# Cross-attention on one core: side work laid out over nearly every key tile, and the scores of a tile behind one wait

## The reference

```
xq  = (1 + scale_q) * layernorm(x)   + shift_q      scale and shift from silu(cond) @ Wss + bss
xkv = (1 + scale_kv)* layernorm(ctx) + shift_kv
q = xq @ Wq + bq                     (4096 x 512, 16 heads of 32)
k, v = xkv @ Wkv + bkv               (3202 x 512 each)
attn = softmax(q @ k^T / sqrt(32))   per head
out = x + (attn @ v) @ Wp + bp
```

## Time and profile before

| | |
|---|---|
| median of 3 runs | 2184.37 us (2181.47 to 2184.44) |
| profiled execution | 2181.79 us, its span 2179.6 us |
| PE busy | 2153.8 us, 99% |
| DVE busy | 1913.6 us, 88% |
| ACT busy | 1817.8 us, 83% |
| exponentials, L1340 | 1600 of 1115 ns, 1692.4 us busy |
| score matmuls, L1091 | 938.3 us busy |
| weigh matmuls, L1103 | 852.3 us busy |

### The profile page before, as it was taken

How to read it: one execution, slowest core, us unless ns; L and a number is a source line. 1 busy time by engine, 2 the same in 40 slices (tenths; PEclk the granted TensorE clock), 3 DMA queues, 4 the chain that set the end, 5 groups by cost and what they waited for, 6 DMA issues and landing times.

```text
span 2179.6 us, 56041 instructions
## 1 busy us (share of the span) xinstructions
PE 2153.8 (99%) x24986; PEld 622.7 (29%) x24986; DVE 1913.6 (88%) x1179; ACT 1817.8 (83%) x1908; POOL 17.3 (1%) x28
## 2 busy tenths in 40 slices
PE   7999999999999999999999999999999999999998
PEld 3444322222222222222222222222222222222222
DVE  2435798899999899999999999999999999989998
ACT  1221899999999999999999999999999999998995
POOL 0001000000000000000000000000000000000000
PEclk9999999999999999999999999999999999999999
DMA  8345522234222422233223322233223322242221
GB/s 297 142 165 181 162 73 56 75 93 115 71 80 77 130 69 77 65 98 109 81 70 99 107 82 69 77 96 106 69 81 89 99 74 77 70 115 83 77 54 51
DMA packets 189011, 210.23 MB, mean 96 GB/s; under 512 B 17238, under 2 KB 120414, under 8 KB 188764
## 3 DMA queue, kind: packets, MB, share of 16 engines
q1 hardware_dynamic: 187180, 206.06, 32.4%
q10 hardware_dynamic: 1584, 0.53, 0.1%
HBM read 169.33 MB, written 37.22 MB: 95 GB/s over the span
## 4 chain that ended last, share of the span: by engine, by line
PE 96%; DVE 1%; issue 1%; ACT 1%; DMA 0%; POOL 0%; SPq 0%; ACTq 0%; DVEq 0%
PE bank L1091 40%; PE bank L1103 36%; PE bank L1120 4%; PE bank L1171 4%; PE bank L1009 4%; PE bank L1020 4%; PE bank L1133 1%; PE bank L1146 1%; PE bank L1229 1%; PE bank L989 1%; ACT arena L1340 1%; DVE stats L1440 0%; DVE arena L1648 0%; PE bank L1156 0%; DVE arena L1454 0%
## 5 line engine op out<-in xcount | busy, mean ns | idle before, releaser
L1340 ACT ACTIVATE arena<-bank,shift 128x1024 f32<-128x1024 f32 x1600 | 1692.4, 1115 | 156.8 <-PE bank L1091 145.6
L1648 DVE TENSOR_TENSOR arena<-arena 128x2048 f32<-128x2048 f32 x736 | 1656.5, 2287 | 113.4 <-ACT arena L1340 105.0
L1091 PE MATMUL bank<-qs,ks 32*64 32x512 f32 x12800 | 938.3, 613 | 1.1 <-ACT arena L1301 0.7
L1103 PE MATMUL bank<-arena,vg 128*32 128x512 f32 x6400 | 852.3, 605 | 1.1 <-ACT arena L1340 1.1
L1091 PEld LDWEIGHTS bank<-qs,ks 32*64 32x64 f32 x12800 | 216.1, 129 | 380.4 <-issue 197.2
L1103 PEld LDWEIGHTS bank<-arena,vg 128*32 128x32 f32 x6400 | 125.9, 108 | 650.4 <-ACT arena L1340 649.6
L1171 PE MATMUL bank<-wp,arena 128*32 128x168 f32 (+2 forms) x2464 | 153.6, 321 | 0.0
L1120 PE MATMUL bank<-xt,wq 128*32 128x256 f32 x1792 | 137.7, 379 | 0.0
L1171 PEld LDWEIGHTS bank<-wp,arena 128*32 128x32 f32 x2464 | 80.0, 110 | 184.4 <-issue 163.9
L1301 ACT ACTIVATE arena<-bank,bk_c 128x512 f32<-128x512 f32 (+1 forms) x28 | 18.0, 642 | 129.9 <-PE bank L1009 129.9
L1120 PEld LDWEIGHTS bank<-xt,wq 128*32 128x32 f32 x1792 | 58.2, 110 | 134.1 <-issue 118.1
(11 more groups left out here) (88 smaller groups left out, 418.9 us busy)
## 6 DMA issues: line engine op xcount, KB each, us to landing
ks<-k_full SPq DMA_DIRECT2D x160, 320.0 KB, 3.1
vg<-v_full SPq DMA_DIRECT2D x160, 320.0 KB, 3.9
p_b<-p_tails SPq DMA_DIRECT2D x128, 128.0 KB, 4.1
arena<-in_x_dram SPq DMA_DIRECT2D x13, 1024.0 KB, 8.1
q_full<-qs SPq DMA_DIRECT2D x32, 256.0 KB, 2.0
out_dram<-arena SPq DMA_DIRECT2D x32, 256.0 KB, 2.0
arena<-l_recip SPq DMA_DIRECT2D x28, 256.0 KB, 5.6
arena<-in_ctx_dram SPq DMA_DIRECT2D x6, 1024.0 KB, 13.5
```

Of the source, the lines that this page charges most:

```text
L1091: mm = nc.tensor.matmul(bank[out, 2 * (i % RING) + h % 2, :], ks[rows_of(h), keys], qs[rows_of(h), g, :], start=True, stop=True)
L1103: mm = nc.tensor.matmul(bank[rows_of(h), o_bank(u), :], vg[:, t, rows_of(h)], pt[t % PR][:, h, :], start=(t == 0), stop=False, skip_group_ ...
L1340: nc.scalar.activation(pt[t % PR][:, 2 * pair:2 * pair + 2, :], bank[:, first:first + 2, :], ACT.Exp, scale=SCALE, bias=shift[:, g:g + 1]) ...
L1648: nc.vector.tensor_tensor(a[:, :, :], (pt[t - 1] if k <= 2 else a)[:, :, :], pt[t % PR][:, :, :], ALU.add).then_inc(p_added, 1)
```

## The change

It has two parts. The first lays out the side work of units with g > 0 anew. In blocks 1 to 6 the first third of the output projection goes to tiles 0, 0, 1 and 2 (two slots in tile 0), both denominator halves to tile 3, the other thirds to tiles 4 to 11, and the queries of the next block, now in thirds of 176, 168 and 168 columns instead of halves of 256, to tiles 12 to 23. In block 0 the queries stay in halves for the eviction, but each half is computed in two parts of 128 columns, in 16 tiles instead of 8, and the denominators go from tiles 4 and 5 to tiles 8 and 9. In block 7 the layout is as before. The evictions follow one tile after the last slot of each job. Units with g = 0 keep their side work. The second part is in `scores`: instead of one wait for each pair of heads, there is one wait ahead of all eight matmuls, for the exponential that frees the banks of the second pair.

```diff
--- before.py
+++ after.py
@@ schedule @@
+            def output_slots(b, g):
+                if b == 0:
+                    return ()
+                if b == NB - 1:
+                    return (0, 1, 2, 3), (6, 7, 8, 9), (10, 11, 12, 13)
+                return (0, 0, 1, 2), (4, 5, 6, 7), (8, 9, 10, 11)
+            def sums_slots(b, g):
+                return (8, 9) if b == 0 else (4, 5) if b == NB - 1 else (3, 3)
+            def query_slots(b):
+                if b == 0 or b == NB:
+                    return ()
+                if b == 1:
+                    return (0, 1, 2, 3, 4, 5, 6, 7), (10, 12, 13, 14, 16, 17, 18, 19)
+                return (12, 13, 14, 15), (16, 17, 18, 19), (20, 21, 22, 23)
+            def query_cols(b, i, part, parts):
+                cuts = OUT_CUTS if b > 1 else (0, HB, QB)
+                a, n = cuts[i], cuts[i + 1] - cuts[i]
+                return slice(a + part * n // parts, a + (part + 1) * n // parts)
+            def last_query(b, m):
+                return "q", b, m, len(query_slots(b)) - 1 if m < NG - 1 else 1
@@ schedule(), the jobs of a unit with g > 0 @@
-                            if b > 0:
-                                jobs.append(("y", b - 1, g, 0))
-                            jobs.append(("l", u - 1))
-                            if b > 0:
-                                jobs.extend(("y", b - 1, g, i) for i in (1, 2))
-                            if b + 1 < NB:
-                                jobs.extend(("q", b + 1, g - 1, i) for i in range(2))
+                            last = {("y", b - 1, g, i): s[-1] for i, s in enumerate(output_slots(b, g))}
+                            last.update({("q", b + 1, g - 1, i): s[-1] for i, s in enumerate(query_slots(b + 1))})
+                            last["l", u - 1] = sums_slots(b, g)[-1]
+                            jobs.extend(sorted(last, key=last.get))
@@ store_q, and the wait of scores() at t == 0 @@
-                            sp.wait_ge(job_taken, JOB["q", b, m, 1] + 1)
+                            sp.wait_ge(job_taken, JOB[last_query(b, m)] + 1)
...
@@ scores() @@
                         for pair in range(2):
                             i = n + pair
-                            if i >= RING:
-                                pe.wait_ge(e_done, i - RING + 1)
+                            if pair == 0 and n + 1 >= RING:
+                                pe.wait_ge(e_done, n + 1 - RING + 1)
@@ project_queries() @@
-                    def project_queries(u, b, m, half, k):
+                    def project_queries(u, b, m, i, n, cols, last):
...
+                        k = n % FT
                         for c in range(HG):
                             col = m * P + c * DH
-                            mm = nc.tensor.matmul(bank[rows_of(c), side_bank(u), halves_of(half)], wq[:, k, col:col + DH],
-                                                  xt[:, k, halves_of(half)], start=(k == 0), stop=(k == FT - 1),
+                            mm = nc.tensor.matmul(bank[rows_of(c), side_bank(u), cols], wq[:, k, col:col + DH],
+                                                  xt[:, k, cols], start=(k == 0), stop=(k == FT - 1),
                                                   skip_group_check=True)
@@ later_side() of TensorE, units with g > 0 @@
-                        if b > 0:
-                            if t < 4:
-                                output(u, b - 1, g, 0, t)
-                            if 6 <= t < 10:
-                                output(u, b - 1, g, 1, t - 6)
-                            if 10 <= t < 14:
-                                output(u, b - 1, g, 2, t - 10)
-                        if 4 <= t < 6:
-                            denominators(u, u - 1, t - 4)
-                        if b + 1 < NB:
-                            if 14 <= t < 18:
-                                project_queries(u, b + 1, g - 1, 0, t - 14)
-                            if 18 <= t < 22:
-                                project_queries(u, b + 1, g - 1, 1, t - 18)
+                        for i, slots in enumerate(output_slots(b, g)):
+                            for k in range(NG):
+                                if t == slots[k]:
+                                    output(u, b - 1, g, i, k)
+                        for half in range(2):
+                            if t == sums_slots(b, g)[half]:
+                                denominators(u, u - 1, half)
+                        for i, slots in enumerate(query_slots(b + 1)):
+                            if t in slots:
+                                n = slots.index(t)
+                                cols = query_cols(b + 1, i, n // FT, len(slots) // FT)
+                                project_queries(u, b + 1, g - 1, i, n, cols, t == slots[-1])
@@ ScalarE, units with g > 0 @@
+                                for i, slots in enumerate(output_slots(b, g)):
+                                    if t == slots[-1] + 1:
+                                        take_output(u, b - 1, g, i)
+                                if t == sums_slots(b, g)[-1] + 1:
                                     take_denominators(u, u - 1)
...
+                                for i, slots in enumerate(query_slots(b + 1)):
+                                    if t == slots[-1] + 1:
+                                        take_queries(u, b + 1, g - 1, i, query_cols(b + 1, i, 0, 1))
```

More of the change, by code:

```diff
@@ L1079, in scores @@
                         if t == 0 and u >= NG:
-                            pe.wait_ge(job_taken, JOB["q", u // NG, g, 1] + 1)
+                            pe.wait_ge(job_taken, JOB[last_query(u // NG, g)] + 1)
                         if t % CT == 0:
@@ L1112, in free @@
                             pe.wait_ge(v_taken, V_JOBS)
-                    def project_queries(u, b, m, half, k):
-                        job = ("q", b, m, half)
-                        if k == 0:
+                    def project_queries(u, b, m, i, n, cols, last):
+                        job = ("q", b, m, i)
+                        if n == 0:
                             free(job)
+                        k = n % FT
                         for c in range(HG):
                             col = m * P + c * DH
-                            mm = nc.tensor.matmul(bank[rows_of(c), side_bank(u), halves_of(half)], wq[:, k, col:col + DH],
-                                                  xt[:, k, halves_of(half)], start=(k == 0), stop=(k == FT - 1),
+                            mm = nc.tensor.matmul(bank[rows_of(c), side_bank(u), cols], wq[:, k, col:col + DH],
+                                                  xt[:, k, cols], start=(k == 0), stop=(k == FT - 1),
                                                   skip_group_check=True)
-                        if k == FT - 1:
+                        if last:
                             mm.then_inc(job_done, 1)
@@ L1179, in first_side @@
                             if t < 4:
-                                project_queries(u, b, 3, 0, t)
+                                project_queries(u, b, 3, 0, t, halves_of(0), t == FT - 1)
                             if 4 <= t < 6:
@@ L1183, in first_side @@
                             if 6 <= t < 10:
-                                project_queries(u, b, 3, 1, t - 6)
+                                project_queries(u, b, 3, 1, t - 6, halves_of(1), t - 6 == FT - 1)
                             if 16 <= t < 20:
@@ L1344, in finished, with take_queries @@
                         act.wait_ge(job_done, DONE[job] + 1)
-                    def take_queries(u, b, m, half):
-                        finished(("q", b, m, half))
+                    def take_queries(u, b, m, i, cols):
+                        finished(("q", b, m, i))
                         act.wait_ge(q_out[m], 16 * b)
-                        nc.scalar.activation(qs[:, m, halves_of(half)], bank[:, side_bank(u), halves_of(half)],
+                        nc.scalar.activation(qs[:, m, cols], bank[:, side_bank(u), cols],
                                              ACT.Identity, bias=bq_c[:, m:m + 1]).then_inc(job_taken, 1)
@@ L1392, in _ @@
                                 if b > 0 and t == 4:
-                                    take_queries(u, b, 3, 0)
+                                    take_queries(u, b, 3, 0, halves_of(0))
                                 if b > 0 and t == 6:
@@ L1396, in _ @@
                                 if b > 0 and t == 10:
-                                    take_queries(u, b, 3, 1)
+                                    take_queries(u, b, 3, 1, halves_of(1))
                                 if b + 1 < NB and t == 11:
@@ L1408, in _ @@
                             else:
-                                if b > 0 and t == 4:
-                                    take_output(u, b - 1, g, 0)
-                                if t == 6:
+                                for i, slots in enumerate(output_slots(b, g)):
```

(6 more changed lines are left out.)

## The result

The changed kernel took 2227.4 us (median of 4 runs, 2227.1 to 2228.3) against 2184.0 for the kernel before: 1.0206 times as long, interval 1.0193 to 1.0218. Forecast were 2220 and slower, with a range of 2196 to 2230. One of the four runs of the last experiment took 2667.9 us at a mean granted clock of 0.753, for a reason that is not known, and is left out; every other run named here had 0.998 or more.

The account below looks back on a forecast made before the run. It took a within-tile loop of scores, exponential and release, 2.407 us, to bound the changed kernel's tiles; the per-unit terms add 36.8 us to 2181.79, 2218.6, put at 2220 (1.6% slower), range 2196 to 2230.

Parts of the forecast that it names:

- The joint wait and the floor of 2.407: Scores: all eight matmuls wait for their tile's first exponential, 1.23 plus 1.17 us, so no tile is shorter than 2.407.
- rival A: Scores' wait: the loop is shorter than read, below 2.33 us, giving 2171 or 2153 us in all; chance 0.11.
- B: Scores' wait, half the price: loop near 2.36 us, only tiles without side work pay, 2192 us; chance 0.07.
- The old loops over two tiles: Kernel before, exponential to weigh to next scores: 4.41 us per two tiles, 4.70 with 168 columns of side work.
- The layout costs nothing: Side work: query thirds take 3.42 us of PE per unit against 3.44 for halves, so equal.
- the two-slot tile: Tile 0 of middle units, two output projection slots: 2.04 + 0.59 = 2.63 us, hiding its eviction.
- The earlier denominators: Tile 3: VectorE's last combining add ends with over 5 us of slack, so moving them earlier costs nothing.
- SP's later store of the queries: SP's queue: store after tile 24 instead of 22; the key load behind it waits for the last weigh anyway; nothing.
- The sum: All units, each tile the greater of 2.407 and PE's work: together +36.8 us on 2181.79, giving 2218.6.
- 18 middle units: Units with g>0 of blocks 1 to 6: 60.89 us against 59.90, +0.99 each, +17.8 together.
- unit 0: First unit, from its first exponential to the next unit's: 61.66 us against 57.67, +4.0.
- Rival C: TensorE's clock falls in small idle times; one tile in ten at the lower level adds 160 us, 2380; chance 0.02.

Follow-up runs that it names:

- the last experiment: Changed kernel with the order of the two waits before a key chunk's first scores turned round, exponential first, keys second: 2219.4 us, 1.0166 of the kernel before.

## Why the prediction was right, and where it fell short

- **The joint wait and the floor of 2.407.** Right: 2.40 to 2.41 in tiles with none, 128 and 168 columns. The latencies had been read from tiles in which the wait existed for half of the scores only; they did not change when all eight waited, which was rival A's hope. The waits are put down to the exponential before 616 of the 800 groups of scores; most of the rest are those with two waits, since with the turned order it is 728. That disposes of A, and the 2.40 disposes of B, which had 2.36.
- **The old loops over two tiles.** Right, by the layout alone (4.70), and by the exponential cut in two (half of 0.16 per tile).
- **The layout costs nothing.** Right for the changed kernel, where the floor hides it (the two-slot tile is 2.64). By itself it gains 4.5 us, and there the two-slot tile, which the prediction's rival A also had at 2.63, is 2.93. The earlier denominators were not late, L1162, their line, waited for ScalarE's evictions, 8.4 us in all, and never for VectorE; SP's later store of the queries and the evictions cost nothing that I could see.
- **The sum.** Mis-sized: 36.8 us forecast, 43.4 measured by the medians (45.9 by the spans). By kind of unit, in us (the first stage gave 0.2 back):

| | forecast | by the traces |
|---|---|---|
| 18 middle units | 17.8 | 23.0 |
| units 1 to 3 | 6.7 | 7.6 |
| unit 0 | 4.0 | 5.5 |
| six g=0 units | 0 | 1.1 |
| unit 28 | 0.8 | 1.0 |
| units 29 and 30 | 5.2 | 6.0 |
| unit 31 to the end | 2.3 | 1.9 |

The term that was too small is the tile that begins a chunk of keys. The prediction's step "no tile can be shorter than 2.40 to 2.41 us, whatever PE has to do" took the wait on the exponential to be the same in all tiles, and in every fifth there is a second wait. With it a middle unit gained 1.27 us instead of 0.99, a unit of block 0 2.52 instead of 2.24, and the g=0 units, forecast unchanged, 0.16 (62.84 to 63.00; their tiles of 2.47 become 2.50). The turned order takes 8 us off, and what is left over the kernel before in the same session is 35.9 us, where the forecast has 36.8. The profile of before could not show the 0.09: there neither of the two waits before the first pair is on the path, because the weigh ahead of it in the queue has already waited for the same exponential. The other part of the miss is unit 0, where the sum took the floor for its first tiles. Its first two take 6.05 us (226.15 to 232.20), 4.38 before (226.37 to 230.75), and not 4.81:

```profile
226.15 1.12 PE L1118 MATMUL bank<-qs,ks 32*64 32x512 f32 x16 [0.66 <-ACT arena L1328]
228.62 1.79 PE L1118 MATMUL bank<-qs,ks 32*64 32x512 f32 x16 [1.35 <-ACT arena L1367]
...
232.20 1.15 PE L1118 MATMUL bank<-qs,ks 32*64 32x512 f32 x16
```

- **The clock.** Rival C did not come: TensorE has up to 0.36 us without work in each tile of 2.40 now (2.40 less the 2.04 of scores and weigh; the profile itself shows up to 0.29 before the scores), through 2 ms, and the granted clock stays at the higher of its two levels (0.999 on average). The Trainium skill (TensorE: Matmul & The Clock Gate, section on psum-queue depth-cycling) tells of another kernel, in bf16, in which small idle times between groups of matmuls made the clock fall and rise again; this trace, at 0.999, does not show that.

The version that beats both kernels, the kernel before by 0.2%, is the layout with the two waits of before, 2176.96 us.

## What to carry to other kernels

Before putting several waits into one, write down the loop that each closes: wait, producer's latency, consumer's latency, back to the wait. The earlier of two waits may close a loop over two tiles and the later one over one tile; joined, the short loop governs, and its length, read from starts in the trace, is a floor under every iteration whatever the engine's work. Where two waits stand before one instruction and one of them is on the path, look in the trace which of the two sits on the instruction itself.

## What the runs showed of the hardware that was not expected

- Two semaphore waits ahead of one TensorE instruction cost 0.09 us when the one released last is the separate instruction (1.26 from the exponential's start to the scores instead of 1.17), and nothing when it is the weight load that waits for it. It does so when the other wait is for keys that have landed (449.62) and when it is for queries (598.17). Of the two waits the one written last became the separate instruction, in the changed kernel and in the one with the turned order.
- The latencies of the loop repeat to 0.01 us in the tiles shown: 1.23 to 1.24 from scores to exponential, 1.17 from exponential to scores, whether four or eight matmuls were released.
- An exponential over 1024 columns, cut into 256 and 768, takes 0.16 us more until its release: tiles went from 2.40 to 2.56.
